# Masked queries of the attentions without rotation: written by ScalarE from the bank, not copied by VectorE

## The chip, the core and the metric

One core of a Trainium2 chip runs the whole program: TensorE (PE), VectorE (DVE), ScalarE (ACT), GpSimd (POOL), SyncE (SP) and the DMA queues. The metric is device time in microseconds (us) of one execution, as the median of several.

## The reference

Four transformer layers over 32 sequences of 128 tokens and 128 features, with a context of the same shape. Each layer is an attention of 16 heads of 8 features and a feed-forward part:

```python
x = x + L0_xattn(layernorm(x), ctx, ctx)   # causal, biases on q, k, v, o
x = x + L0_ffn(layernorm(x))               # 8 experts, top 2, relu
x = x + L1_xattn(layernorm(x), ctx, ctx)   # no mask, biases
x = x + L1_ffn(layernorm(x))               # 8 experts, top 2, gelu
x = x + L2_xattn(layernorm(x), ctx)        # causal self (L2a), then over ctx (L2b), then dense ffn
x = x + L2_ffn(layernorm(x))               # gated: 8 experts that are attentions
x = x + L3_xattn(layernorm(x), ctx, ctx)   # rotated q and k, window of 64
x = x + L3_ffn(layernorm(x))               # 8 experts, top 2, silu gate
```

In each attention `scores = q k^T / sqrt(8)` per head, a softmax, and the weighted sum of v. L0 and L1 have a bias on the query (`q = x Wq + bq`), L2's two attentions have none.

## The kernel before

The 32 sequences are two streams of 16; a stream goes through its sequences in 8 pairs (256 tokens), stage by stage: L0 for all pairs, L0's experts over 39 tiles, L1 for all pairs, L1's experts, then for each pair all of L2 and L3's attention, and L3's experts. The program is written by hand for five engines. The steps of both streams are interleaved on every engine in one order, which `choose_order` (L144) makes beforehand from costs and delays that PE's steps yield; each engine then executes in that order without looking ahead. Semaphores release: `filled` of a bank when PE has written it, `taken` of a bank when its last reader is done, and named ones per stream. So an instruction that waits holds back the other stream's work behind it on its engine.

PSUM has eight banks in rings (`RINGS`). The ring "g", banks 4 to 7, serves both streams in turn: projections, the scores of which maxima are taken, sums and transposes; `open_bank` (L340) waits until the bank's last use is taken. 

One attention without rotation (L0, L1, L2a, L2b; 64 in all) runs like this. PE projects the query into one bank ("q"; in L2a the key goes into the same bank). ACT's `queries` (L1083) reads that bank twice: into `qb` in bf16, then into `qf` in f32 (half of the tile `qfs`), and in L2a also the key into `kf`; then the bank is given back. Heads lie in 4 bands of 32 partitions, 4 heads of 8 rows in each. To pick single heads, DVE's `split` (L1384) makes four copies, each times a column of 0 and 1 from `band`: of the key into `km` (bf16, `split_keys`), of the query into `qm` (f32, `begin`). PE's `scores` (L403) multiplies `qb` and `km` into ring g for the maxima that DVE takes (`mx`, L1531); `scores_t` (L426) multiplies `kf` and `qm` into banks 0 to 3, takes the maxima off, and ACT's exps follow. In `attention` (L1563) DVE first waits until the query's bank is taken, copies, and only then goes on to the next step in the order, which as a rule is the other stream's: `tail_turned` and `turned` (tiles `tail_tok`, `h_tok`), `values` (`vaug`), maxima or, in the gated attention, `eq` tiles (L1626).

L3's attention rotates the query on DVE and keeps `qf`, its copies and its semaphores.

Of the kernel before, what the change touches and what calls it, by code (L numbers as in the profile page):

```python
# [100 lines left out]
PROJ = ["L0q", "L0k", "L0v", "L0o", "L1q", "L1k", "L1v", "L1o", "L2q1", "L2k1", "L2v1", "L2q2", "L2k2",  # L101
        "L2v2", "L3q", "L3qs", "L3k", "L3ks", "L3v", "L3o"] + [f"E{m}{p}" for p in range(HP) for m in "qkvo"]
COLS = ["L0q", "L0k", "L1q", "L1k", "L3q", "L3qs", "L3k", "L3ks"] + [f"E{m}{p}" for p in range(HP) for m in "qk"] \
    + [f"f1{c}" for c in range(CH)]
ROWS = ["L0v", "L0o", "L1v", "L1o", "L2v1", "L2v2", "L3v", "L3o", "g1", "be1", "g2", "be2", "g3", "be3",
        "bf2"]
ROUTERS = {0: 0, 1: 1, 3: 2}
# [68 lines left out]
def build(nc, A, out, totals):  # L176
    with ExitStack() as ctx:
# [153 lines left out]
        def _(pe):  # L331
# [8 lines left out]
            def open_bank(ring, *key):  # L340
                i, n = banks.fill(ring, key)
                if w.new(f"taken{i}", n - 1):
                    pe.wait_ge(sem[f"taken{i}"], n - 1)
                return bank[i]
# [4 lines left out]
            def taken(*key):  # L349
                i, n = banks.fills[key]  # L350
                if w.new(f"taken{i}", n):
                    pe.wait_ge(sem[f"taken{i}"], n)

            def stream(s):
# [46 lines left out]
                def attend(k, mask, rot=False, tail=None):  # L401
# [3 lines left out]
                    def scores(b, j):  # L405

                        if b == j == 0:
                            pe.wait_ge(sem[f"keys_ready{s}"], w.next(f"keys_ready{s}"))
                            if rot:
                                pe.wait_ge(sem[f"queries_ready{s}"], w.next(f"queries_ready{s}"))  # L410
                            else:
                                taken(*k, "q")
                        ps = [open_bank("g", *k, "s", b, j + i) for i in range(2)]
                        for i in range(2):
                            r = band_rows(j + i)
                            mm = nc.tensor.matmul(ps[i][:], qb[s][r, seq(b)], km[s][r, :, seq(b)], start=True,  # L416
                                                  stop=mask is None)
                            if mask is None:
                                filled(mm, *k, "s", b, j + i)
                        if mask is not None:  # L420
                            for i in range(2):
                                filled(nc.tensor.matmul(ps[i][:], identb[:, 0, :], masks[:, 2 * mask, :].unsqueeze(1)  # L422
                                                        .to_broadcast([P, HB, P]), start=False, stop=True),
                                       *k, "s", b, j + i)

                    def scores_t(b):  # L426
                        if b == 0:
                            pe.wait_ge(sem[f"split_ready{s}"], w.next(f"split_ready{s}"))
                        ps = [open_bank("t", *k, "sT", b, j) for j in range(BANDS)]
                        for j in range(BANDS):  # L430
                            nc.tensor.matmul(ps[j][:], kf[s][band_rows(j), seq(b)], qm[s][band_rows(j), :, seq(b)],  # L431
                                             start=True, stop=False)
                        if mask is not None:
                            for j in range(BANDS):
                                nc.tensor.matmul(ps[j][:], identb[:, 0, :], masks[:, 2 * mask + 1, :].unsqueeze(1)
                                                 .to_broadcast([P, HB, P]), start=False, stop=False)
                        for j in range(BANDS):
                            taken(*k, "s", b, j)
                            for i in range(HB):
                                h = HB * j + i  # L440
                                mm = nc.tensor.matmul(ps[j][:, i * P:(i + 1) * P],  # L441
                                                      mx[s][:, b, h:h + 1].to_broadcast([P, P]), identb[:, 1, :],
                                                      start=False, stop=i == HB - 1)
                            filled(mm, *k, "sT", b, j)
# [608 lines left out]
        def _(act):  # L1053
# [12 lines left out]
            def stream(s):  # L1066
# [15 lines left out]

                def queries(k, name, bias, rot=False, keys_too=False):  # L1083
                    ps = take(*k, "q")
                    if not rot:
                        shifted(qb[s][:], ps[:, 0:NT], name if bias else None)
                    ins = shifted(qf[s][:], ps[:, 0:NT], name if bias else None)
                    if rot:
                        ins = shifted(qs[s][:], ps[:, NT:2 * NT], name + "s" if bias else None)
                    if keys_too:  # L1090
                        ins = shifted(kf[s][:], ps[:, NT:2 * NT], None)
                    give(ins, *k, "q")

                def exp(i, last_read, *key):
# [204 lines left out]
        def _(dve):  # L1299
# [35 lines left out]
            def stream(s):  # L1335
# [218 lines left out]
                    yield "unit"  # L1554
                    divide(1)

                def begin():
                    split(qm, qf).then_inc(sem[f"split_ready{s}"], 1)

                def split_keys():  # L1560
                    split(km, kf).then_inc(sem[f"keys_ready{s}"], 1)

                def attention(k, x, bias, rot=False, tail=None):  # L1563
                    taken(*k, "q")
                    if rot:
                        rotate(qf)
                        nc.vector.tensor_copy(qb[s][:], qf[s][:]).then_inc(sem[f"queries_ready{s}"], 1)
                    begin()
                    yield "q"
                    yield from attend(k, tail)  # L1570
                    yield "unit"
                    settle(nc.vector.tensor_tensor(x[:], x[:], row(bias), ALU.add))
                    yield "att"
                    ps = take(*k, "out")
                    settle_given(nc.vector.tensor_tensor(x[:], x[:], b2(ps[:, 0:NT]), ALU.add), *k, "out")
                    norm(x, 1)
                    yield "out"
# [150 lines left out]
                for i in range(PAIRS):  # L1728
# [7 lines left out]
                    turned(x)  # L1736
                    yield "turns"
                    values(k, "L2v1")
                    taken(*k, "q")
                    split_keys()  # L1740
                    begin()
                    yield "q"
                    yield from attend(k, tail)
                    settle(nc.vector.tensor_tensor(hh[:], h[:], att_tok[s][:], ALU.add))
# [6 lines left out]
                    yield "kv"  # L1751
                    turned(hh, gain=row("g1"), shift=row("be1"))
                    yield "turn"
                    taken(*k, "q")
                    begin()
                    yield "q"
                    yield from attend(k)
                    settle(nc.vector.tensor_tensor(hh[:], h[:], att_tok[s][:], ALU.add))
# [46 lines left out]
def laid_out(i):  # L1805
# [28 lines left out]
        col[f"Eq{e}"], col[f"Ek{e}"] = pairs(f["L2_ffn_qb"])[e], pairs(f["L2_ffn_kb"])[e]  # L1834
    for c in range(CH):
        col[f"f1{c}"] = f["L2_xattn_bf1"][c * P:(c + 1) * P]
    row = {"L0v": f["L0_xattn_bv"], "L0o": f["L0_xattn_bo"], "L1v": f["L1_xattn_bv"], "L1o": f["L1_xattn_bo"],
           "L2v1": f["L2_xattn_bv1"].reshape(P), "L2v2": f["L2_xattn_bv2"].reshape(P), "L3v": f["L3_xattn_v_b"],
           "L3o": f["L3_xattn_o_b"], "bf2": f["L2_xattn_bf2"]}
# [35 lines left out]
        .astype(np.float32)  # L1875
    own = np.arange(P)[:, None] // D % NE == np.arange(NE)[None, :]
    a["vbias"] = np.where(own[:, None, :], pairs(f["L2_ffn_vb"]).T[:, :, None], 0.0).astype(np.float32)
    a["band"] = (np.arange(P)[:, None] % 32 // D == np.arange(HB)[None, :]).astype(np.float32)
    a["tri"] = (np.arange(NE)[None, :] < np.arange(NE)[:, None]).astype(np.float32)
    for n in (0, 1, 3):  # L1880
        a[f"moe{n}"] = a[f"moe{n}"].reshape(NE * P, -1)
# [25 lines left out]
```

## Time and profile before

| | |
|---|---|
| time, 3 runs | 3804.05, 3807.44, 3823.59 us; median 3807.44 |
| profiled execution | 3820.63 us; its span 3818.7 us |
| PE / DVE / ACT / POOL busy | 2878.4 / 2028.2 / 1361.3 / 639.8 us |
| L0, both streams: period of a pair of each | 47.6 us (copies at 252.15 and 299.74) |
| L1, the same | 50.4 us (copies at 849.34 and 899.70) |
| L2, gated attention and L3, the same | 279.9 us (copies at 2004.61 and 2284.50) |

The profile is of one execution on the only core. The timeline lists instructions in order of their start in microseconds, merges neighbours of a kind with a count, and says in brackets how long the engine had been idle before and what released it. Rows of LDWEIGHTS are not used.

### The profile page before, as it was taken

The numbers are of one execution on the slowest core, as the hardware profiler recorded it, in microseconds if no ns is written. First come the engines' busy times: TensorE is split into PE (matmuls) and PEld (weight loads), VectorE is DVE, ScalarE is ACT, GpSimd is POOL, SyncE is SP. The second block draws the span as 40 slices with busy tenths as digits, with TensorE's granted clock in tenths as the row PEclk, the third lists the DMA queues.
The fourth block names the chain that finished last, engine by engine and source line by source line (L and its number), as shares of the span: only waits on it lengthen the run. The fifth ranks groups of instructions, "written<-read, shape, count | busy, mean of one in ns | idle before, by whom it ended". The sixth has DMA issues, their size and how long they took to land. (4 is left out here: it accounts for less than half of the span.)

```text
span 3818.7 us, 62592 instructions
## 1 busy us (share of the span) xinstructions
PE 2878.4 (75%) x23570; PEld 2120.4 (56%) x23570; DVE 2028.2 (53%) x6834; ACT 1361.3 (36%) x3026; POOL 639.8 (17%) x853
## 2 busy tenths in 40 slices
PE   5887867665777877878878878878878878959453
PEld 2344646533565755746746746746646646738352
DVE  3566344466444356656656556556656566554411
ACT  1333323232554733323323324324334333327210
POOL 1122111233211011111111111111111111110303
PEclk8778989876988988978979979979879889879776
DMA  6201535300544500000000000000000000014353
GB/s 231 100 23 49 175 120 173 103 25 23 179 145 146 156 9 7 2 8 7 2 8 7 2 9 5 3 8 5 4 10 2 4 9 2 2 36 128 96 144 102
DMA packets 146506, 216.98 MB, mean 57 GB/s; under 512 B 20376, under 2 KB 99232, under 8 KB 146080
## 3 DMA queue, kind: packets, MB, share of 16 engines
q1 hardware_dynamic: 133920, 187.79, 16.2%
q0 software_dynamic: 12288, 25.19, 2.3%
q8 instruction: 190, 3.11, 0.3%
q14 instruction: 108, 0.88, 0.1%
HBM read 159.82 MB, written 53.08 MB: 56 GB/s over the span
## 5 line engine op out<-in xcount | busy, mean ns | idle before, releaser
L1099 ACT ACTIVATE ex<-bank 128x512 f32<-128x512 f32 x896 | 483.3, 601 | 675.6 <-PE bank L441 453.1
L1531 DVE TENSOR_REDUCE mx<-bank 128x4 bf16<-128x512 f32 x640 | 406.7, 684 | 82.8 <-PE bank L422 44.4
L927 POOL TENSOR_TENSOR rstd<-vare,power 128x2 f32<-128x2 f32 x192 | 138.6, 722 | 1378.9 <-DVE vare L1350 1378.4
L936 POOL DMA_INDIRECT sent<-tail_tok,pos x192 | 192.4, 1002 | 601.2 <-DVE pos L1472 557.9
L368 PE MATMUL bank<-hT,wproj 128*128 128x256 f32 x736 | 275.2, 477 | 12.5 <-ACT hT L1069 12.2
L991 POOL TENSOR_TENSOR oT<-oT 128x128 f32<-128x128 f32 x256 | 118.5, 463 | 952.3 <-DVE oT L1644 952.2
L524 PE MATMUL bank<-qm,expert 128*128 128x128 f32 x1872 | 273.4, 293 | 2.0 <-ACT ex L1099 1.4
L596 PE MATMUL bank<-ev,ex 128*128 128x65 f32 x2048 | 271.4, 277 | 0.0
L596 PEld LDWEIGHTS bank<-ev,ex 128*128 128x128 f32 x2048 | 263.9, 196 | 6.1
L524 PEld LDWEIGHTS bank<-qm,expert 128*128 128x128 f32 x1872 | 252.5, 209 | 6.4 <-issue 6.2
L358 PE MATMUL bank<-ident,h_tok 128*128 128x128 f32 x224 | 69.0, 406 | 233.1 <-DVE h_tok L1361 124.7
L416 PE MATMUL bank<-km,qb 32*128 32x512 bf16 x640 | 148.5, 473 | 125.1 <-DVE mx L1531 49.2
L532 PE MATMUL bank<-expert,hid 128*128 128x128 f32 x1560 | 232.1, 291 | 5.7 <-ACT ex L1099 3.3
L431 PE MATMUL bank<-qm,kf 32*128 32x512 f32 x1280 | 217.4, 740 | 22.8 <-ACT ex L1099 12.8
L1632 DVE TENSOR_REDUCE emax<-bank 128x4 bf16<-128x512 f32 x256 | 175.2, 687 | 90.1 <-PE bank L571 89.1
L516 PE MATMUL bank<-ident,qm 128*128 128x128 f32 x234 | 77.3, 331 | 191.9 <-DMA qm<-sent 191.4
L580 PE MATMUL bank<-qm,ek 128*128 128x256 f32 x768 | 219.6, 412 | 0.6
L532 PEld LDWEIGHTS bank<-expert,hid 128*128 128x128 f32 x1560 | 210.7, 207 | 9.2 <-ACT ex L1099 6.0
L441 PEld LDWEIGHTS bank<-identb,mx 128*128 128x128 bf16 x2560 | 157.0, 100 | 77.8 <-issue 55.6
L1523 DVE RECIPROCAL rden<-bank 128x16 f32<-128x16 f32 x160 | 41.0, 256 | 279.1 <-PE bank L460 277.4
L451 PE MATMUL bank<-ex,vaug 128*9 128x128 f32 x5120 | 175.9, 275 | 8.6 <-DVE mx L1531 6.4
L358 PEld LDWEIGHTS bank<-ident,h_tok 128*128 128x128 f32 x224 | 29.8, 186 | 266.3 <-DVE h_tok L1361 137.1
(200 smaller groups left out, 5376.4 us busy)
## 6 DMA issues: line engine op xcount, KB each, us to landing
expert<-in_moe SPq DMA_DIRECT2D x78, 578.0 KB, 4.0
expert<-in_moe SPq DMA_DIRECT2D x78, 512.0 KB, 3.8
expert<-in_moe SPq DMA_DIRECT2D x78, 384.0 KB, 3.3
sent<-zeros SPq DMA_DIRECT2D x8, 2560.0 KB, 8.6
qm<-sent SPq DMA_DIRECT2D x234, 64.0 KB, 3.6
answered<-qm SPq DMA_DIRECT2D x234, 64.0 KB, 3.4
ctxT<-ctx_kept SPq DMA_DIRECT2D x32, 128.0 KB, 2.1
wproj<-in_wproj SPq DMA_DIRECT2D x1, 3328.0 KB
```

The source lines that it names most:

```text
L368: mm = nc.tensor.matmul(ps[:, n * NT:(n + 1) * NT], W(weight), src[:], start=True, stop=True)
L431: nc.tensor.matmul(ps[j][:], kf[s][band_rows(j), seq(b)], qm[s][band_rows(j), :, seq(b)], start=True, stop=False)
L441: mm = nc.tensor.matmul(ps[j][:, i * P:(i + 1) * P], mx[s][:, b, h:h + 1].to_broadcast([P, P]), identb[:, 1, :], start=False, stop=i == HB ...
L451: mm = nc.tensor.matmul(ps[32 * i:32 * i + D + 1, j * P:(j + 1) * P], vaug[s][:, b, HB * j + i, :], ex[s][:, j, i, :], start=True, stop=True)
L524: mm = nc.tensor.matmul(ps[:, chunk(c)], expert[s][:, t % SLOTS, chunk(c)], t_turned[s][:, t % 2, :], start=True, stop=True)
L532: mm = nc.tensor.matmul(ps[:, 0:P], t_hid[s][:, t % 2, chunk(c)], expert[s][:, t % SLOTS, 512 + c * P:512 + (c + 1) * P], start=c == 0, st ...
L580: nc.tensor.matmul(out_[:, :, i, :], ek[p % 3][s][:, i, seq(b)], eq[s][p % 3][:, :, seq(b)], start=i == 0, stop=False)
L596: mm = nc.tensor.matmul(ps[:, i * (HE + 1):(i + 1) * (HE + 1)], ex[s][:, u % 4, i, :], ev[s][:, p % 2, b, i % 2, :], start=True, stop=True)
L936: nc.gpsimd.indirect_dma_start(sent[s][:], bass.IndirectOffsetOnAxis(ap=pos[s][:, i, j:j + 1], axis=0), tail_tok[s][:, j // 2, :], None).t ...
L1099: give(nc.scalar.activation(ex[s][:, i], ps[:].rearrange("p (i q) -> p i q", i=4), ACT.Exp, scale=SCALE), *key)
L1531: give(nc.vector.tensor_reduce(mx[s][:, b, HB * i:HB * i + HB], ps[:].rearrange("p (i k) -> p i k", i=HB), AX.X, ALU.max), *k, "s", b, i)
L1632: give(nc.vector.tensor_reduce(emax[s][:, u % 4, :], ps[:].rearrange("p (i k) -> p i k", i=4), AX.X, ALU.max), *k, "s", u)
```

## The change

In `queries` without rotation ACT writes `qb` first and signals `queries_ready`, then writes the four masked queries `qm` itself from the bank: each an ACTIVATE with a column of `band` as per-partition scale, in L0 and L1 with a bias that is masked the same way (eight new columns of constants, `L0q0` to `L1q3`), in L2 as Copy with a scale. The bank is given back after the fourth. In L2a the key is read first. DVE's copies of the query and its wait for the bank go; in L2a DVE waits for `queries_ready` before it copies the key. PE's first scores wait for `queries_ready`, and `scores_t` for the bank to be taken.

```diff
@@ PE, scores and scores_t
-                            if rot:
-                                pe.wait_ge(sem[f"queries_ready{s}"], w.next(f"queries_ready{s}"))
-                            else:
-                                taken(*k, "q")
+                            pe.wait_ge(sem[f"queries_ready{s}"], w.next(f"queries_ready{s}"))
...
-                        if b == 0:
+                        if b == 0 and rot:
                             pe.wait_ge(sem[f"split_ready{s}"], w.next(f"split_ready{s}"))
+                        elif b == 0:
+                            taken(*k, "q")
@@ ACT, queries
                     ps = take(*k, "q")
-                    if not rot:
-                        shifted(qb[s][:], ps[:, 0:NT], name if bias else None)
-                    ins = shifted(qf[s][:], ps[:, 0:NT], name if bias else None)
                     if rot:
-                        ins = shifted(qs[s][:], ps[:, NT:2 * NT], name + "s" if bias else None)
+                        shifted(qf[s][:], ps[:, 0:NT], name)
+                        give(shifted(qs[s][:], ps[:, NT:2 * NT], name + "s"), *k, "q")
+                        return
                     if keys_too:
-                        ins = shifted(kf[s][:], ps[:, NT:2 * NT], None)
+                        shifted(kf[s][:], ps[:, NT:2 * NT], None)
+                    shifted(qb[s][:], ps[:, 0:NT], name if bias else None).then_inc(sem[f"queries_ready{s}"], 1)
+                    for h in range(HB):
+                        if bias:
+                            ins = nc.scalar.activation(qm[s][:, h, :], ps[:, 0:NT], ACT.Identity, bias=col(f"{name}{h}"),
+                                                       scale=band[:, h:h + 1])
+                        else:
+                            ins = nc.scalar.activation(qm[s][:, h, :], ps[:, 0:NT], ACT.Copy, scale=band[:, h:h + 1])
                     give(ins, *k, "q")
@@ DVE, attention
-                    taken(*k, "q")
+                    w.next(f"queries_ready{s}")
                     if rot:
+                        taken(*k, "q")
                         rotate(qf)
                         nc.vector.tensor_copy(qb[s][:], qf[s][:]).then_inc(sem[f"queries_ready{s}"], 1)
-                    begin()
+                        split(qm, qf).then_inc(sem[f"split_ready{s}"], 1)
@@ DVE, L2a
-                    taken(*k, "q")
+                    dve.wait_ge(sem[f"queries_ready{s}"], w.next(f"queries_ready{s}"))
                     split_keys()
-                    begin()
@@ DVE, L2b
-                    taken(*k, "q")
-                    begin()
+                    w.next(f"queries_ready{s}")
```

How the order moves, at three places (`filled5`: bank 5 written, `taken5`: bank 5 given back). On ACT in the L0 stage, both streams: a query of one stream and the load of the other, before:

```order
L1069 ACTIVATE attT<-bank 128x256 [waits filled6]
L1069 ACTIVATE hT<-bank 128x256 [waits filled7]
L1074 ACTIVATE qb<-bank,cols 128x256 [waits filled5]
L1074 ACTIVATE qfs<-bank,cols 128x256
L1069 ACTIVATE ctxT<-bank 128x256 [waits filled6,ctx_kept0]
L1074 ACTIVATE kf<-bank,cols 128x256 [waits filled7]
```

and now:

```order
L1068 ACTIVATE attT<-bank 128x256 [waits filled6]
L1068 ACTIVATE hT<-bank 128x256 [waits filled7]
L1073 ACTIVATE qb<-bank,cols 128x256 [waits filled5]
L1093 ACTIVATE qm<-bank,cols,band 128x256 x4
L1068 ACTIVATE ctxT<-bank 128x256 [waits filled6,ctx_kept0]
L1073 ACTIVATE kf<-bank,cols 128x256 [waits filled7]
```

One instruction has become four, ahead of the other stream's ctxT. On DVE in the L1 stage, both streams: the tail and the query of stream 0, then the same of stream 1 and its first maxima, before:

```order
L1356 TENSOR_SCALAR h_tok<-x_tok,mv,rstd 128x128
L1386 TENSOR_SCALAR qm<-qfs,band 128x256 [waits taken4,ln_ready0]
L1386 TENSOR_SCALAR qm<-qfs,band 128x256 x3
L1356 TENSOR_SCALAR tail_tok<-x_tok,mv,rstd 128x128 [waits rstd_ready1,scattered1]
L1356 TENSOR_SCALAR tail_tok<-x_tok,mv,rstd 128x128
L1356 TENSOR_SCALAR h_tok<-x_tok,mv,rstd 128x128 [waits rstd_ready1]
L1356 TENSOR_SCALAR h_tok<-x_tok,mv,rstd 128x128
L1531 TENSOR_REDUCE mx<-bank 128x4 [waits filled7,ln_ready1]
L1531 TENSOR_REDUCE mx<-bank 128x4 [waits filled4]
L1386 TENSOR_SCALAR qm<-qfs,band 128x256 [waits taken5]
L1386 TENSOR_SCALAR qm<-qfs,band 128x256 x3
L1531 TENSOR_REDUCE mx<-bank 128x4 [waits filled7]
```

and now:

```order
L1361 TENSOR_SCALAR h_tok<-x_tok,mv,rstd 128x128
L1361 TENSOR_SCALAR tail_tok<-x_tok,mv,rstd 128x128 [waits rstd_ready1,scattered1,ln_ready0]
L1361 TENSOR_SCALAR tail_tok<-x_tok,mv,rstd 128x128
L1361 TENSOR_SCALAR h_tok<-x_tok,mv,rstd 128x128 [waits rstd_ready1]
L1361 TENSOR_SCALAR h_tok<-x_tok,mv,rstd 128x128
L1536 TENSOR_REDUCE mx<-bank 128x4 [waits filled7,ln_ready1]
L1536 TENSOR_REDUCE mx<-bank 128x4 [waits filled4]
L1536 TENSOR_REDUCE mx<-bank 128x4 [waits filled7]
```

Both sets of copies and both waits for a query's bank (taken4, taken5) are gone from between the two streams' work. PE's instructions stand as before; only the semaphores of the first scores and of `scores_t` differ. One place of it in the L2 stage now, where stream 1's query (L2b) goes into bank 5 and two pairs of stream 0's L3 scores follow:

```order
L358 MATMUL bank<-ident,h_tok 128x128 [waits taken4,ln_ready1]
L358 MATMUL bank<-ident,h_tok 128x128
L368 MATMUL bank<-hT,wproj 128x256 [waits taken5,taken4]
L413 MATMUL bank<-km,qb 128x512 [waits taken7,taken6]
L413 MATMUL bank<-km,qb 128x512
L419 MATMUL bank<-masks,identb 128x512 x2
L413 MATMUL bank<-km,qb 128x512 [waits taken5]
L413 MATMUL bank<-km,qb 128x512
```

The same rows stood there before: the second pair of scores waits for bank 5, which the query holds.

## Rows read from the trace of the kernel before

**Rows 1.** Cores: span and mean granted TensorE clock.
```profile
core 0: 3818.7 us, clock 0.853
```

**Rows 2.** Windows (bounds, length; busy us and instructions by engine; PEclk, DMA share, GB/s): L1, L2.
```profile
750.00:950.00 200.00, 119.87 (x1224) 76.03 (x1222) 133.34 (x490) 60.40 (x130) 63.64 (x69) 0.71 0.08 23
...
1953.00:2233.00 280.00, 228.57 (x1831) 167.38 (x1830) 168.61 (x548) 97.19 (x210) 41.88 (x64) 0.87 0.02 6
```

**Rows 3.** Groups (busy us, mean ns | idle before, releasers): the query copies on DVE.
```profile
L1386 DVE TENSOR_SCALAR qm<-qfs,band 128x256 f32<-128x256 f32 x320 | 91.8, 351 | 80.1 <-ACT qfs L1074 48.7 <-ACT qfs L1073 31.3
```

**Rows 4.** One tile (ns min/median/max, first and last start, form): ACT's bf16 query.
```profile
L1074 ACT ACTIVATE qb<-bank,cols x32: 474/474/475, 36.4 to 1111.3; 128x256 bf16<-128x256 f32 x32
...
L1073 ACT ACTIVATE qb<-bank x32: 384/384/384, 1149.8 to 3362.9; 128x256 bf16<-128x256 f32 x32
```

**Rows 5.** Timeline (start, us, instruction, count [idle before <-releaser]), L0, both streams.
```profile
298.86 0.47 ACT L1074 ACTIVATE qb<-bank,cols 128x256 bf16<-128x256 f32 x1 [1.32 <-PE bank L368]
...
299.24 0.47 ACT L1074 ACTIVATE qfs<-bank,cols 128x256 f32<-128x256 f32 x1
...
299.59 0.38 ACT L1069 ACTIVATE ctxT<-bank 128x256 f32<-128x256 f32 x1
...
299.74 1.14 DVE L1386 TENSOR_SCALAR qm<-qfs,band 128x256 f32<-128x256 f32 x4 [0.23 <-ACT qfs L1074]
...
300.03 1.22 PE L368 MATMUL bank<-ctxT,wproj 128*128 128x256 f32 x2 [0.78 <-ACT ctxT L1069]
```

**Rows 6.** Timeline, L0, one stream alone: the first scores.
```profile
104.54 0.61 PE L416 MATMUL bank<-km,qb 32*128 32x512 bf16 x2 [0.98 <-issue]
```

**Rows 7.** Timeline, ACT, L0, the other attention of the period.
```profile
269.92 2.07 ACT L1099 ACTIVATE ex<-bank 128x512 f32<-128x512 f32 x4 [3.29 <-PE bank L441]
```

**Rows 8.** Timeline, L0 beside the other stream's expert tiles.
```profile
451.34 0.47 ACT L1074 ACTIVATE qb<-bank,cols 128x256 bf16<-128x256 f32 x1 [0.73 <-PE bank L368]
...
455.43 0.33 PE L516 MATMUL bank<-ident,qm 128*128 128x128 f32 x1 [0.85 <-DMA qm<-sent]
```

**Rows 9.** Timeline, L1, both streams.
```profile
898.75 0.47 ACT L1074 ACTIVATE qb<-bank,cols 128x256 bf16<-128x256 f32 x1 [1.31 <-PE bank L368]
...
899.70 1.14 DVE L1386 TENSOR_SCALAR qm<-qfs,band 128x256 f32<-128x256 f32 x4 [3.49 <-ACT qfs L1074]
...
901.40 0.69 PE L358 MATMUL bank<-ident,tail_tok 128*128 128x128 f32 x2 [2.69 <-DVE tail_tok L1356]
...
902.54 0.61 PE L416 MATMUL bank<-km,qb 32*128 32x512 bf16 x2
...
904.34 0.47 ACT L1074 ACTIVATE qb<-bank,cols 128x256 bf16<-128x256 f32 x1 [1.31 <-PE bank L368]
...
906.27 1.28 DVE L1531 TENSOR_REDUCE mx<-bank 128x4 bf16<-128x512 f32 x2
```

**Rows 10.** Timeline, PE: waits for maxima behind a full DVE queue.
```profile
1162.40 0.61 PE L416 MATMUL bank<-km,qb 32*128 32x512 bf16 x2 [7.03 <-DVE mx L1531]
...
1366.40 0.39 PE L416 MATMUL bank<-km,qb 32*128 32x512 bf16 x2 [0.78 <-DVE mx L1531]
```

**Rows 11.** Timeline, L2b beside the other stream's L3.
```profile
1963.79 0.38 ACT L1073 ACTIVATE qb<-bank 128x256 bf16<-128x256 f32 x1 [1.31 <-PE bank L368]
...
1965.19 0.61 PE L416 MATMUL bank<-km,qb 32*128 32x512 bf16 x2
```

**Rows 12.** Timeline, L2a beside the other stream's dense layer.
```profile
2002.83 1.95 PE L736 MATMUL bank<-wf,hid 128*128 128x128 f32 x16
...
2005.66 0.41 DVE L1768 TENSOR_TENSOR hh_tok<-hh_tok,bank 128x256 f32<-128x256 f32 x1
...
2007.82 0.39 PE L416 MATMUL bank<-km,qb 32*128 32x512 bf16 x2 [1.80 <-DVE mx L1531]
```

**Rows 13.** Timeline, L2b beside the start of the gated attention.
```profile
2038.09 0.38 ACT L1073 ACTIVATE qb<-bank 128x256 bf16<-128x256 f32 x1 [0.58 <-PE bank L368]
...
2038.85 1.14 DVE L1386 TENSOR_SCALAR qm<-qfs,band 128x256 f32<-128x256 f32 x4 [0.72 <-ACT qfs L1073]
...
2040.80 0.39 PE L416 MATMUL bank<-km,qb 32*128 32x512 bf16 x2 [0.89 <-DVE qm L1626]
```

More of the change, by code:

```diff
@@ L103 @@
 COLS = ["L0q", "L0k", "L1q", "L1k", "L3q", "L3qs", "L3k", "L3ks"] + [f"E{m}{p}" for p in range(HP) for m in "qk"] \
-    + [f"f1{c}" for c in range(CH)]
+    + [f"f1{c}" for c in range(CH)] + [f"{n}{i}" for n in ("L0q", "L1q") for i in range(HB)]
 ROWS = ["L0v", "L0o", "L1v", "L1o", "L2v1", "L2v2", "L3v", "L3o", "g1", "be1", "g2", "be2", "g3", "be3",
@@ L1555, in attend @@
                     divide(1)
-                def begin():
-                    split(qm, qf).then_inc(sem[f"split_ready{s}"], 1)
                 def split_keys():
@@ L1836, in laid_out @@
         col[f"f1{c}"] = f["L2_xattn_bf1"][c * P:(c + 1) * P]
+    in_band = np.arange(P)[:, None] % 32 // D == np.arange(HB)[None, :]
+    for n in ("L0q", "L1q"):
+        for h in range(HB):
+            col[f"{n}{h}"] = np.where(in_band[:, h], col[n], 0.0).astype(np.float32)
     row = {"L0v": f["L0_xattn_bv"], "L0o": f["L0_xattn_bo"], "L1v": f["L1_xattn_bv"], "L1o": f["L1_xattn_bo"],
@@ L1877, in laid_out @@
     a["vbias"] = np.where(own[:, None, :], pairs(f["L2_ffn_vb"]).T[:, :, None], 0.0).astype(np.float32)
-    a["band"] = (np.arange(P)[:, None] % 32 // D == np.arange(HB)[None, :]).astype(np.float32)
+    a["band"] = in_band.astype(np.float32)
     a["tri"] = (np.arange(NE)[None, :] < np.arange(NE)[:, None]).astype(np.float32)
```

## Prediction

> **What bounds the kernel now.** I read the core's span and clock first, then the costliest groups, the windows by stage, and last the timeline of all engines around every one of the 64 attentions without rotation (16 each of L0 and L1, 32 of L2). The span is 3818.7 us at a granted clock of 0.853 [rows 1], the execution took 3820.63 us. The windows say that no engine is full: in L1's stage TensorE (PE) is busy 60% and VectorE (DVE) 67%, in one period of the L2 stage 82% and 60%, ScalarE (ACT) only 30 to 35% [rows 2]. So the time is a chain that changes engines, and what an instruction is worth depends on whether the chain passes it. The four query copies on DVE are 320 instructions in all, 256 of them without rotation; DVE sat idle 80.1 us waiting for ACT's query before them [rows 3]. That wait blocks what is queued behind it for the other stream; this, more than the copies' length, is what the change can win.
>
> **Prices.** Four DVE copies in a row take 1.14 us [rows 5]; the change takes 64 such rows away, 73 us of DVE's time. On ACT one output of 128x256 takes 474 ns with a bias operand and 384 ns without [rows 4]. Neighbours overlap by 0.10 us: the bank's second reader starts 0.38 us after the first, not 0.47 [rows 5]. A copy with a per-partition scale and bias stands nowhere in this trace. An operand costs at most what the bias row shows, 90 ns, and at least nothing; I take 90 ns for each, being the nearest row: 0.56 us for a copy in L0 and L1 (steps of 0.46), 0.47 us in L2 (steps of 0.37). From the start of the first output to the end of the last read of the query's bank, L0 and L1 go from 0.37 + 0.47 = 0.84 us to 0.37 + 3 x 0.46 + 0.56 = 2.31 us, **1.47 us more**; L2 from 0.28 + 0.38 = 0.66 to 0.28 + 3 x 0.37 + 0.47 = 1.86 us, **1.20 us more**. With operands for nothing these are 1.11 and 0.84, with no overlap about 1.9 and 1.6. ACT gets about 85 us of work. The order of the work, the bank ring and all DMAs stay; eight more columns of constants are loaded once and count as nothing behind the other loads.
>
> The Trainium skill (ScalarE: Activation LUTs, What ACT_TABLE_LOAD costs) says each per-partition pointer operand adds about 93 ns to an ACTIVATE. By it the copies come out within a few hundredths of a microsecond of mine, and the sum within 1 us; no row here has two such operands.
>
> **The 64 places, by pattern.** (a) Single-stream L0, 4 times. PE waits for the whole query before its first scores [rows 6]; now it waits for the bf16 copy alone, 0.37 us earlier, and the masked copies are done before its second pair. **-1.5 us.**
>
> (b) L0 with both streams, the attention followed by the other stream's load, 4 times. ACT's ctxT evacuation stands right behind the query, and PE already waits 0.78 us for it [rows 5]. It goes back by 1.47 us; all that follows (keys, the key copies on DVE, the maxima, the other stream's tail_tok for which PE waits) hangs on it. The DVE time freed there buys nothing, since DVE waits for PE next. **+5.9 us.**
>
> (c) The other L0 attention of that period, 4 times: ACT has 3.29 us free before its next exps [rows 7], and PE runs without a gap. Nothing.
>
> (d) L0, L1 and L2 beside the other stream's expert tiles, 7 times: PE's next tile waits for its rows by DMA until 455.43; ACT's delayed tile evacuation is done before that (the query starts at 451.34, + 2.31 + 0.28 = 453.9) [rows 8]. If that cover were gone, each would cost up to 1.47 us. Nothing.
>
> (e) L1 with both streams, 3 periods. DVE waits 3.49 us for ACT's query, copies, and only then makes tail_tok and h_tok for the other stream, for which PE has waited 2.69 us [rows 9]. Now DVE makes them at once. What is late next is the query's bank: the ring of four comes round to it with the first scores. It is returned at 898.75 + 2.31 + 0.1 = 901.2 against 902.54 before, so 1.4 us are won. Then the second query, at 904.34 before and now near 903.1, no longer puts its copies ahead of the maxima at 906.27, which can start near 904.0 when their scores are there; PE next waits for the second query's bank, returned at 903.1 + 2.4 = 905.5. In all 2.1 us are won per period. **-6.3 us.**
>
> (f) A saturated DVE queue with PE waiting for maxima at its end, 3 times (two of them stand in [rows 10], the third is like the first): the copies come off in full, -1.14 us twice, or as far as the wait goes, -0.8 us. **-3.1 us.** Four attentions in odd places at the ends of stages I read as -0.7, +0.5 and -0.4 together: **-0.6 us.** The rest of the L1 places are covered by these or by (d).
>
> (g) L2b beside the other stream's L3 scores, 8 times. DVE's copies are hidden. The fourth score bank after the query is the query's own: it comes back at 1963.79 + 1.86 + 0.1 = 1965.75, and PE wanted it at 1965.19 [rows 11]. This is a new wait of PE on ACT with exps and maxima behind it. **+4.5 us.**
>
> (h) L2a beside the dense layer, 7 times. DVE's four copies end where it takes hh_tok at 2005.66. Without them it takes it at about 2005.0, 0.2 us after PE's dense product is done (2002.83 + 1.95); the maxima for which PE waits 1.80 us come 0.7 us sooner [rows 12]. **-4.9 us.**
>
> (i) L2b beside the start of the gated attention, 7 times. The copies at 2038.85, after another wait of 0.72 us on ACT, hold back the other stream's eq tile of L1626, for which PE waits 0.89 us [rows 13]. Now PE is bound by the query's bank, 2038.09 + 1.86 + 0.1 = 2040.05 against 2040.80: **-5.2 us.**
>
> (j) L2a inside the gated attention, 7 times, and the L2 places before the steady state: the copies stood between maxima that PE reaches later, and ACT is free. Nothing.
>
> **The sum:** -1.5 + 5.9 - 6.3 - 3.1 - 0.6 + 4.5 - 4.9 - 5.2 = **-11.2 us**, from 3820.63 to 3809.4. The profiled execution is 13.2 us above the median of the runs shown, so I put the median at 3807.44 - 11.2 = **3796 us**. With operands for nothing (b) is 4.4, (g) 1.6, (e) -7.4 and (i) -7.7: -19 us. Without overlap they are 7.5, 7.7, -5.0 and -2.4: -2 us.
>
> **Rivals.** *More comes back than the waits.* PE's clock fell in the stretches with DVE waits: 0.71 in the L1 window [rows 2], where a pair of score matmuls takes 0.61 us [rows 9] against 0.39 us at the upper of the two levels (1.2 and 2.4 GHz) [rows 13]. PE was idle for 2.69 us before those slow ones, and it is at the upper level where it had run without such a gap. If fewer gaps let a third of the 120 us of PE's busy time in that window run at the upper level, that is another 120 / 3 x 0.36 = 14 us, -26 us in all, 3781 us. For it: -2.1 us falls on the very gap before the slow rows. Against: most of the gaps stay (DVE maxima and gates), and (b) and (g) open new ones. Chance 0.22.
>
> *ACT becomes the path; slower.* The query's bank is held 1.2 to 1.47 us longer, in a ring of four that both streams share, and every evacuation behind it is late. I count 12 places where that reaches PE. It decides if it reaches some 30: 30 x 1.35 us = 40, less the 21 us of gains, is +19 us, 3826 us; at all 64 it is +65 us, 3872 us. For it: one wait of this kind is plain in rows 5. Against: ACT is idle two thirds of the time, and I followed each pattern. Chance 0.08. The Trainium skill (ScalarE: Activation LUTs, Rules for kernel authors) says to put multiplies on VectorE, not ScalarE, as VectorE is faster per element; the trace agrees on the speed (four in 1.14 us against my 1.58 to 1.94), and that rule would bring the slower outcome.
>
> *The change wins nothing.* The DVE gains of (e), (h) and (i) are taken by the next wait while (b) and (g) stay: +9 us or less in size, 3808 to 3817 us. For it: in every one of them the bank's return is only 0.7 to 1.4 us ahead of the old time. Chance 0.12.
>
> **How the numbers follow.** The forecast's case, -2 to -19 us, has 0.58. A measurement of this kernel can tell about 0.5% from no change, 19 us. Faster by more than that: the first rival and the tail of the forecast, 0.26. Slower: the second rival, 0.08. Within: 0.66. The range reaches from the first rival, 3779, to 3814, most of the third; about 0.8 lies within.
>
> **What would show it.** Right: DVE's TENSOR_SCALAR qm row falls from 320 to 64, and ACT has 256 new ones of 0.47 and 0.56 us; DVE's wait for qfs (80.1 us) is gone but for the rotated queries; PE's wait of 2.69 us for tail_tok in L1 is replaced by a shorter one for ACT; L1's period (50.4 us) shortens by about 2 us, L0's (47.6 us) lengthens by about 1.5 us, L2's (279.9 us) shortens by about 0.9 us. Wrong: copies of another length, an L2 period that moved by more than 3 us, or a clock that moved by over 0.01.

## The result, and the profile after

The changed kernel takes 3779.12 us (median of 5 runs, 3772.20 to 3782.27) against 3808.95 us before; the ratio is 0.991, 95% interval 0.9887 to 0.9933. The gain is 29.8 us between the medians (34 by the ratio), where 11.2 were forecast. The profiled execution took 3772.20 us (before 3820.63), so the traces differ by 48 us, some 19 more than the medians: the profiled execution of before was a long one.

The page of the changed kernel, its busy times (columns as in part 1 of a page):
```profile
span 3770.3 us, 62550 instructions
PE 2832.7 (75%) x23570; PEld 2087.7 (55%) x23570; DVE 1960.6 (52%) x6578; ACT 1443.4 (38%) x3218; POOL 637.2 (17%) x853
```
The cores view and the groups of the copies, changed kernel (busy us, mean ns | idle before, releaser):
```profile
core 0: 3770.3 us, clock 0.865
...
L1391 DVE TENSOR_SCALAR qm<-qfs,band 128x256 f32<-128x256 f32 x64 | 18.1, 347 | 0.0
...
L1093 ACT ACTIVATE qm<-bank,cols,band 128x256 f32<-128x256 f32 x128 | 61.7, 569 | 0.0
L1096 ACT ACTIVATE qm<-bank,band 128x256 f32<-128x256 f32 x128 | 50.2, 482 | 0.2
```
The moved work is as priced: 0.57 and 0.48 us for a copy on ACT (forecast 0.56 and 0.47). DVE lost 256 copies and the 80.1 us wait ahead of them [rows 3]. ACT is 82 us busier, and PE, whose 23570 instructions did not change, is **46 us less busy** at a clock of 0.865 instead of 0.853 [rows 1]. That last line is the surprise.

The places, in the timeline of the changed kernel (start, us, instruction [idle before <-releaser]). L0 with both streams answers to [rows 5]: PE's wait for ctxT went from 0.78 to 2.24 us, +1.46.
```profile
303.03 1.93 ACT L1093 ACTIVATE qm<-bank,cols,band 128x256 f32<-128x256 f32 x4
...
304.83 0.40 ACT L1068 ACTIVATE ctxT<-bank 128x256 f32<-128x256 f32 x1
...
305.28 1.22 PE L368 MATMUL bank<-ctxT,wproj 128*128 128x256 f32 x2 [2.24 <-ACT ctxT L1068]
```
L1 with both streams answers to [rows 9]: PE's 2.69 us wait for tail_tok is gone, and in its place stands one of 1.63 us for the query's bank. From ACT's start on the query to these scores it is 2.44 us instead of 3.79 [rows 9], 1.35 won against 1.34 forecast.
```profile
892.18 0.63 PE L358 MATMUL bank<-ident,tail_tok 128*128 128x128 f32 x2
892.43 0.47 ACT L1073 ACTIVATE qb<-bank,cols 128x256 bf16<-128x256 f32 x1 [1.31 <-PE bank L368]
...
892.80 1.93 ACT L1093 ACTIVATE qm<-bank,cols,band 128x256 f32<-128x256 f32 x4
...
894.87 0.61 PE L413 MATMUL bank<-km,qb 32*128 32x512 bf16 x2 [1.63 <-ACT qm L1093]
```
The three places of L2, for [rows 11], [rows 12] and [rows 13]: a new wait of 0.43 us, then 1.00 instead of 1.80 us, then 0.20 instead of 0.89 us.
```profile
1937.05 0.60 PE L413 MATMUL bank<-km,qb 32*128 32x512 bf16 x2 [0.43 <-ACT qm L1096]
...
1977.91 0.42 DVE L1769 TENSOR_TENSOR hh_tok<-hh_tok,bank 128x256 f32<-128x256 f32 x1 [0.24 <-PE bank L735]
...
1980.08 0.39 PE L413 MATMUL bank<-km,qb 32*128 32x512 bf16 x2 [1.00 <-DVE mx L1536]
...
2012.45 0.80 PE L413 MATMUL bank<-km,qb 32*128 32x512 bf16 x4 [0.20 <-ACT qm L1096]
```
Each of these places moved as forecast, to within 0.15 us. The sum did not. To see where it failed I set the two traces side by side at the 192 rstd instructions of POOL, which are the same in both, and took the time from one to the next:

| stage, in the time of before | forecast | changed kernel less before | five runs without a change in L0 or L1, less before |
|---|---|---|---|
| 0 to 161, L0, one stream | -1.5 | -0.4 | -2.4 to +1.8 |
| 161 to 348, L0, both | +5.9 | **+6.0** | -1.6 to +0.5 |
| 348 to 736, beside expert tiles | 0 | -5.5 | -4.4 to -1.6 |
| 736 to 946, L1, both | -6.3 | -9.6 | -2.2 to +0.7 |
| 946 to 1353, beside expert tiles; L2 begins | up to -3.7, (f) and odd places | -10.2 | -9.8 to -1.8 |
| one L2 period (279.9) | -0.9 | **-4.4 or -2.4 in turn** | (L2 was changed in them) |
| 3403 to the end, no attention without rotation | 0 | -4.1 | -6.6 to +3.3 |

The last column (runs e5, e6, e15_s0, e15_s1 and e16, below; from 1150 us on they differ in an L2 attention) shows what a stage varies by with unchanged code: several us beside the expert tiles, where transfers set the pace, and always downwards from the long profiled execution of before. L2's periods vary by 0.3 to 0.4 us at most once they have settled (one of e15_s1 was 3.2 us short), so there the 24 us over seven periods are real. Windows over two L2 periods, from the same rstd instruction to itself two periods on, first before, then changed:
```profile
2007.16:2566.95 559.79, 456.95 (x3660) 334.80 (x3660) 337.03 (x1093) 194.40 (x420) 84.02 (x128) 0.87 0.02 6
```
```profile
1979.42:2532.37 552.95, 449.35 (x3660) 329.61 (x3660) 329.44 (x1061) 203.88 (x444) 83.57 (x128) 0.89 0.02 6
```
The pair of periods is 6.84 us shorter. PE's busy time (second number) fell by 7.60 us with the same 3660 instructions, its idle time rose by 0.76. What L2 gained is faster matmuls; over the whole period its waits did not get shorter.

### The profile page after: what moved, and what is told of

It is laid out like the page before. It is cut to its first block and busy times, and to the rows that moved or that the text cites. A ratio compares the mean times of both kernels' runs of the same rounds, so it can differ in the third digit from the quotient of the medians.

```text
span 3770.3 us, 62550 instructions
## 1 busy us (share of the span) xinstructions
PE 2832.7 (75%) x23570; PEld 2087.7 (55%) x23570; DVE 1960.6 (52%) x6578; ACT 1443.4 (38%) x3218; POOL 637.2 (17%) x853
## 5 line engine op out<-in xcount | busy, mean ns | idle before, releaser
L368 PE MATMUL bank<-hT,wproj 128*128 128x256 f32 x736 | 263.5, 459 | 14.1 <-ACT hT L1068 13.8
L523 PEld LDWEIGHTS bank<-qm,expert 128*128 128x128 f32 x1872 | 244.4, 203 | 6.4 <-issue 6.1
L440 PE MATMUL bank<-identb,mx 128*128 128x128 bf16 x2560 | 179.6, 226 | 0.0
```

The source lines that it names most:

```text
L368: mm = nc.tensor.matmul(ps[:, n * NT:(n + 1) * NT], W(weight), src[:], start=True, stop=True)
L440: mm = nc.tensor.matmul(ps[j][:, i * P:(i + 1) * P], mx[s][:, b, h:h + 1].to_broadcast([P, P]), identb[:, 1, :], start=False, stop=i == HB ...
L523: mm = nc.tensor.matmul(ps[:, chunk(c)], expert[s][:, t % SLOTS, chunk(c)], t_turned[s][:, t % 2, :], start=True, stop=True)
```

## The experiments

Two theories. **Places**: the time is the sum of the waits at the places of the prediction. **Clock**: a small saving also lets PE run more of its work at the upper of its two levels, and this decides. The runs were made in groups, each on one chip beside its own runs of before: e1 to e4, e5 to e8, e9 with e12, e13 to e15, and e16. Gains of a run in us are its ratio times the time of before, unless a trace is named. The snippets are shortened, and names such as `wproj_248_columns` stand for longer expressions.

**Stages apart (e1, e2, e3).** A condition on the layer decides on all engines whether the masked queries come from ACT or, as before, from DVE:
```diff
+BY_ACT = ("L0", "L1")                 # e2: ("L2a", "L2b"); e3: ("L1", "L2a", "L2b")
-    if rot:                            # DVE, attention()
+    if k[2] not in BY_ACT:
         taken(*k, "q")
+        begin()                        # the four copies
```


> The change in L0 and L1 alone (128 of the 256 copies on ACT); L2's attentions as before. By the places of the prediction: -1.5 + 5.9 - 6.3 - 3.1 - 0.6 = -5.6 us against before (ratio 0.9985). By the theory that TensorE's clock gives back more at many places in every stage (the traces of the two kernels differ by 20 us at 1353 us): -10 to -20 us (0.997 to 0.995), with L2's period back at 279.9 us.

> The change in L2 alone (the other 128 copies). By the places of the prediction: +4.5 - 4.9 - 5.2 = -5.6 us (0.9985), an L2 period of 279.0 us. By the clock theory: L2's period falls by about 3.5 us as in the changed kernel, -17 to -24 us (0.9955 to 0.9935), and PE's busy time in a period falls by as much as the period, while its idle time stays.

> The change in L1 and L2, L0 as before. If the late ctxT evacuation of L0 with both streams costs what the prediction and the trace say (+5.9 us less the 1.5 us won in single-stream L0), this is 4.4 us faster than the changed kernel: 3775 us, ratio to before 0.990. If L0's stage beside expert tiles gained on its own (the traces say up to -7 us from 380 to 736 us), it is 0 to 3 us slower than the changed kernel.

L0 and L1 alone: 0.9986 (0.9976 to 0.9997), -5.3 us where the places say -5.6. L2 alone: 0.9933 (0.9919 to 0.9947), -25.5 us where they say -5.6. The parts add up to the whole. Without L0: 0.9901 (0.9884 to 0.9918), in the direction of the 4.4 us that L0 costs, though the interval reaches the changed kernel; the trace is clearer: stage 161 to 348 is 6.0 to 6.4 us longer in e1, e7 and both traces of the changed kernel (4.5 in e4), and +0.4 us in e3. So L0 and L1 were read right, and a term of L2 is far off.

**DVE's wait or DVE's copies (e4, e7).** e4 keeps a wait of DVE on ACT's query, e7 keeps copies:
```diff
+    dve.wait_ge(sem[f"queries_ready{s}"], n)        # e4: where taken(*k, "q") stood
```
```diff
+    for i in range(HB):                             # e7: where the copies stood, no wait
+        nc.vector.tensor_scalar(spare[:, s, i, :], wproj_248_columns, band[:, i:i + 1], None, ALU.mult)
```


> The changed kernel, but DVE still waits for ACT's bf16 query at the place where it waited before; no copies on DVE. If DVE's blocking wait carries the gain (the prediction's L1 places), most of it goes: 0 to -8 us against before, L1's period back near 50 us. If the 73 us of copies carry it, most stays: -20 us or more against before, with L2's period as in the changed kernel (276.5 us). By the places of the prediction about 4 us of its 11 go.

> The changed kernel with four DVE products of 128x248 (inputs constants, outputs read by nobody) put where the query's copies were, without a wait: 256 instructions, about 73 us of DVE. If the copies' time carries the gain, most of it goes: 0 to -10 us against before, L2's period back near 279 us. If DVE's blocking wait carried it, the kernel stays at -25 us or better. With the run in which DVE still waits (0.9923) this splits the gain in two.

e4's wait ends with ACT's first output, a little sooner than the wait of before, which was for the bank; and in L2a the changed kernel has it anyway, so e4 tests L0, L1 and L2b. e7's products are of 128x248 instead of 128x256, without a wait. With the wait kept the kernel is at 0.9923 (0.991 to 0.9937): nearly the whole gain stays. With the copies back it is at 0.9975 (0.9958 to 0.9992), and two L2 periods take 559.5 to 559.9 us: L2's gain is gone (PE's wait at the place of [rows 12] is back at 1.70 us). The copies carry it. In L1 either is enough: its stage was 5.9 us shorter in e4 and 7.6 in e7, against 5.3 to 9.6 in runs with both; behind the first relief waits the query's bank.

**Which attention of L2 (e5, e6), which stream (e15).** The same condition, on L2a, on L2b, and on L2a of one stream.

> The change in L2's first attention alone (16 of 64 attentions). By the prediction's places: -0.7 us in each of 7 periods and nothing inside the gated attention, -4.9 us (ratio 0.9987), period 279.2 us. If the step of -1.1 and -2.9 us that the changed kernel shows at the first attention inside the gated one is this attention's own, -2 to -2.7 us per period: -14 to -19 us (0.996 to 0.995). If it is only TensorE's clock answering to the whole period's pattern, no half of the change alone need show its share.

> The change in L2's second attention alone. By the prediction's places: +4.5 - 5.2 = -0.7 us (1.000), period 279.8 us, with the new wait of 0.4 to 0.5 us of PE for the query's bank. If the two halves add up to the 3.45 us per period of the whole, it takes what the other run leaves: -5 to -11 us. If the clock makes it, the halves do not add up, and PE's idle time in a period is within 1 us of before in both.

> The change in L2's first attention of stream 0 alone (8 of 64 attentions). If the place beside the dense layer decides, the stream that has it gives the whole step (two periods 552.9 us, -24 us, ratio 0.9935) and the other nothing. If both places count the same, each gives half of it (556.4 us, -12 us, 0.997).

> The same for stream 1 alone. With its neighbour it adds up to the run of both streams (0.9931) if the two places count by themselves; by a step theory the sum need not hold, and each is 0, -12 or -24 us.

L2a alone: 0.9931 (0.9911 to 0.9951), all of L2's gain. L2b alone: 0.9997 (0.9986 to 1.0008), -1 us, where the places say -0.7. In stream 0 L2a stands beside the other stream's dense layer: 0.9929 (0.9912 to 0.9945). In stream 1 it stands inside the gated attention: 0.9997 (0.9986 to 1.0009). **Eight attentions out of 64, 32 copies, suffice for the whole step**, and they are the places of [rows 12], priced at 0.7 us each. In run e15_s0 the place itself gave just that (1.00 us of waiting against 1.80):
```profile
1991.80 0.42 DVE L1794 TENSOR_TENSOR hh_tok<-hh_tok,bank 128x256 f32<-128x256 f32 x1 [0.24 <-PE bank L739]
...
1993.97 0.39 PE L417 MATMUL bank<-km,qb 32*128 32x512 bf16 x2 [1.00 <-DVE mx L1547]
```
The rest came later in the same period, where no instruction had been changed. Windows of 4 us, kernel before (the number behind the five engines is PEclk):
```profile
2178.00:2182.00 4.00, 2.17 (x18) 1.74 (x16) 2.65 (x9) 1.14 (x3) 0.45 (x1) 1.00 0.00 0
2182.00:2186.00 4.00, 2.02 (x7) 1.41 (x8) 2.27 (x12) 0.77 (x2) 1.16 (x2) 0.61 0.00 0
2186.00:2190.00 4.00, 4.00 (x19) 3.54 (x18) 0.89 (x3) 0.60 (x1) 0.00 (x0) 0.50 0.01 4
2190.00:2194.00 4.00, 4.00 (x17) 3.44 (x17) 1.31 (x5) 1.32 (x4) 0.46 (x1) 0.61 0.01 2
2194.00:2198.00 4.00, 4.00 (x35) 3.26 (x33) 3.29 (x13) 1.58 (x3) 0.45 (x1) 1.00 0.00 0
```
The same stretch in run e15_s0:
```profile
2164.00:2168.00 4.00, 1.54 (x15) 1.26 (x13) 2.58 (x12) 0.98 (x2) 0.05 (x1) 1.00 0.00 0
2168.00:2172.00 4.00, 2.40 (x9) 1.85 (x10) 2.31 (x9) 0.77 (x2) 1.16 (x2) 0.74 0.00 0
2172.00:2176.00 4.00, 4.00 (x28) 3.52 (x27) 0.80 (x3) 1.31 (x4) 0.46 (x1) 0.83 0.01 4
2176.00:2180.00 4.00, 3.89 (x32) 3.22 (x30) 3.71 (x13) 1.67 (x6) 0.00 (x0) 1.00 0.00 0
```
In both PE had been half idle for some 8 us and its clock fell to the lower level (1.2 of 2.4 GHz). Before, it stayed there through one whole window of solid work (0.50) and most of the next (0.61); in e15_s0 it was back in the first third of one (0.83). PE's timeline, before and e15_s0:
```profile
2189.42 1.16 PE L374 MATMUL bank<-wproj,hT 128*128 128x128 f32 x4
2190.38 1.91 PE L368 MATMUL bank<-hT,wproj 128*128 128x256 f32 x4
2192.08 1.06 PE L374 MATMUL bank<-wproj,hT 128*128 128x128 f32 x4
```
```profile
2174.11 0.66 PE L375 MATMUL bank<-wproj,hT 128*128 128x128 f32 x4
2174.61 1.03 PE L369 MATMUL bank<-hT,wproj 128*128 128x256 f32 x4
2175.47 0.61 PE L375 MATMUL bank<-wproj,hT 128*128 128x128 f32 x4
```
The same twelve matmuls took 3.72 us (2189.42 to 2193.14) in the one and 1.97 (2174.11 to 2176.08) in the other, with no wait in either; with their neighbours ahead this stretch gave 2.4 us. A second of this kind, near 2130, gave 1.1 us. With the 0.74 us of the place these make 4.2. Some 0.8 us went back later, partly in longer waits of PE and partly where matmuls came out at the lower level instead: 3.4 us are left, the period's gain. Two periods of e15_s0, to be held against those of before shown above:
```profile
1993.31:2546.24 552.93, 449.25 (x3660) 327.73 (x3660) 334.87 (x1085) 196.56 (x426) 83.59 (x128) 0.90 0.02 6
```
Per period PE is 3.85 us less busy and 0.4 us more idle: the time saved at the place comes back as idle time elsewhere, and the whole gain is in PE's busy time. That the saving is what brought the clock up sooner is inferred from the edit, which touched nothing else; the link between the two was not isolated.

**How the saving turns into time (e9, e12).** e9 puts 1, 2 or 3 idle copies back into L2a alone; e12 is e3 (L0 as before) and gives L2b's bank back early:
```diff
+    for i in range(1):                              # 2, 3; DVE, L2a only, behind split_keys()
+        nc.vector.tensor_scalar(spare[:, s, i, :], wproj_248_columns, band[:, i:i + 1], None, ALU.mult)
```
```diff
+    give(shifted(qf[s][:], ps[:, 0:NT], None), *k, "q")        # e12: ACT, L2b
+    act.wait_ge(sem[f"taken{i}"], n)
+    ... nc.scalar.activation(qm[s][:, h, :], qf[s][:], ACT.Copy, scale=band[:, h:h + 1])
```


> The changed kernel with one idle DVE product of 128x248 (0.33 us) back in each of L2's first attentions. So far L2's period was 279.9 us or 276.5 us in the mean of two, whatever was changed, and nothing between. If the period follows the path (linear theory), four products make 3.4 us and one makes 0.85: 277.3 us. If it moves in one step between two values, it is 276.5 or 279.9 us, here most likely 276.5.

> Two idle products in each of L2's first attentions. Linear theory: 278.2 us. Step theory: 276.5 or 279.9 us in the mean of two periods, and a run time that differs from the neighbour's by 0 or by some 24 us.

> Three idle products in each of L2's first attentions. Linear theory: 279.0 us. Step theory: 276.5 or 279.9 us; once the step has come, a further product costs nothing.

> L0 as before, the change in L1 and L2; in L2's second attention ACT first writes the query's bf16 and f32 forms, gives the bank back (as early as before) and makes the four masked copies from the f32 form. It takes away the new wait of PE for the query's bank (0.43 us, with 1.0 us more idle time per period in the run of L2b alone) and adds 0.28 us to ACT. Linear theory: 1 us per period less than in the kernel without L0, -8 us: 3763 us. Step theory: the period stays at 276.5 us (same time as without L0, 0.990), or goes down a further step of 3.4 us to 273.1 us (-24 us, 0.984).

Two periods of L2 took 556.4 us with one idle copy, 559.8 with two, 559.8 with three. Neither theory as put held: the period is not linear in the work, nor does it have only two values. Nor does it follow the wait that was saved. At the place of [rows 12] PE waited 1.00 us with one idle copy, as with none, 1.18 with two and 1.44 with three, against 1.80 before. Here e9_copies1, then e9_copies2:
```profile
2040.43 0.39 PE L414 MATMUL bank<-km,qb 32*128 32x512 bf16 x2 [1.00 <-DVE mx L1537]
```
```profile
2033.65 0.39 PE L414 MATMUL bank<-km,qb 32*128 32x512 bf16 x2 [1.18 <-DVE mx L1537]
```
The idle copies stand in L2a of both streams, so with one of them the loss must come from elsewhere in the period; where was not followed up. Windows over two periods of e9_copies1, then e9_copies2:
```profile
2039.77:2596.17 556.40, 454.07 (x3660) 332.46 (x3660) 329.80 (x1065) 203.66 (x444) 83.58 (x129) 0.88 0.02 6
```
```profile
2032.99:2592.80 559.81, 457.31 (x3660) 334.53 (x3660) 330.70 (x1069) 204.00 (x444) 83.68 (x129) 0.87 0.02 6
```
The ratios follow: 0.9946 (0.9925 to 0.9967), 0.9983 (0.9973 to 0.9994), 0.9986 (0.9973 to 0.9999); one product of 0.34 us costs half the step, the second the other half, the third nothing. e12 also came out at 556.4 us and 0.993 (0.9914 to 0.9946): taking a wait of 0.43 us away and adding 0.28 us of ACT work did not give a microsecond per period but, against e3's 552.95 us, took half a step back. Over all runs, two settled periods took:

| two periods, us | kernels |
|---|---|
| 559.8 (559.5 to 560.1) | before, e1, e6, e7, e9_copies2, e9_copies3, e15_s1, e16 |
| 556.4 | e9_copies1, e12 |
| 552.9 to 553.2 | changed kernel (twice), e2, e3, e4, e5, e8, e14, e15_s0 |

**Control, and the leanest version (e13, e14).** e9 and e12 ran on a chip whose kernel before took 3851 us, not 3803 to 3810. e13 is the changed kernel unaltered, on another chip; e14 has BY_ACT = ("L1", "L2a").

> The changed kernel once more, as the control of its neighbours. If the chip has no part in the steps, two of L2's periods make 552.9 us again; if the chip decides, 556.4 us or another value, and the ratio to before moves from 0.991.

> The change in L1 and in L2's first attention alone; L0 and L2b as before. It leaves out the two places with a new wait of PE (L0 with both streams, L2b beside the L3 scores). By the steps: two periods of L2 at 552.9 us, ratio near the kernel without L0 (0.990) and 1 us better than it for the L2b wait if that is on the path; next step down: 0.984.

e13: 0.9922 (0.9908 to 0.9936), two periods 552.9 us. The slower chip loses its time ahead of L2 (its two periods of 559.8 us in e9 agree with the others within 0.03 us), so the middle value is probably those kernels' own; the changed kernel itself was not run on that chip. e14: 3775.26 us, 0.991 (0.9892 to 0.9928), beside e13's 3778.66: as good with half of the copies moved, and not measurably better. e3 has the lowest ratio, 0.9901. No version beats the changed kernel beyond the intervals.

**Filling PE's idle time (e8), moving the copies (e16).**
```diff
     for i in range(2):                              # e8: PE, scores()
         ps.append(open_bank("g", *k, "s", b, j + i))
+        if i == 0:
+            nc.tensor.matmul(ps[0][:], identb[:, 0, :], mask_512_columns, start=True, stop=True)
```
```diff
     split_keys()                                    # e16: DVE, kernel before, L2a, stream 0
-    begin()
     yield "q"
+    begin()
```


> The changed kernel with one more product on PE (128x512 bf16, overwritten at once) between the openings of the two score banks of a pair, 320 in all, where PE mostly waits for DVE's maxima. It removes no wait and only fills idle time. If the granted clock decides, it rises above 0.867 and the matmuls behind those waits come out at the upper level: 5 to 40 us faster than the changed kernel. If the clock has no part in it, the kernel is slower by what is not hidden, 0 to 320 x 0.21 = 67 us.

> The kernel before, with all 320 copies on DVE, but in L2's first attention of stream 0 they stand behind the step of the other stream that follows instead of ahead of it. If the 0.7 us at that place decide, the period falls by 3.4 us here too (two periods 552.9 us) and the run is near 0.993, as with the copies on ACT. If DVE's load decides (9 us of copies per stream), nothing changes: 1.000, period 279.9 us.

e8 raised the clock, to 0.869 against 0.865, and was 0.998 (0.9968 to 0.9993): some 25 us slower than the changed kernel. Two L2 periods took 552.95 us all the same, with 8.5 us more of PE's busy time and as much less idle; the loss is in the other stages. A higher clock, bought with this work on PE, did not pay. e16: 1.0011 (0.9999 to 1.0022), no gain. Behind the other stream's step the copies still stand ahead of L2a's maxima, and PE's wait there was 2.01 us, not shorter than 1.80:
```profile
1999.74 0.39 PE L416 MATMUL bank<-km,qb 32*128 32x512 bf16 x2 [2.01 <-DVE mx L1531]
```
This other order does not help; what helped was to take the copies off DVE at that place.

## Why the prediction was wrong

- **Prices**: right. 0.57 and 0.48 us against 0.56 and 0.47; DVE's 256 copies and its wait are gone.
- **(b)** +5.9: right, +6.0 in the stage, +1.46 us of wait at the place against 1.47.
- **(e)** -6.3: right in size, and the next wait was the query's bank, as forecast. The stage gave 5.3 to 9.6 us in the runs with L1 changed, those on the slower chip apart. But the claim that DVE's blocking wait, "more than the copies' length", is what can be won fell: e4 kept a wait on ACT's query and stayed at 0.9923.
- **(a), (d), (f)** and the odd places: L0 and L1 together were -5.3 us against -5.6 forecast. Singly they drown in the scatter of the stages beside expert tiles. At one place near 556 us, by its length the third of (f), priced at -1.14, there is a new wait of 1.26 us for the query's bank that I had not foreseen, ahead of the wait for maxima, which fell from 7.39 to 4.65 us; from ACT's start on the query to the scores behind both it is 7.70 us instead of 8.94, -1.2 us.
- **(g)** +4.5 and **(i)** -5.2: right at the places (0.43 us against 0.56; 0.69 against 0.75), and in sum (e6: -1 us against -0.7).
- **(j)** 0: right (e15_s1, 0.9997).
- **(h)** -4.9, "the maxima for which PE waits 1.80 us come 0.7 us sooner": **the step that failed.** The mechanism and the 0.7 us are right (0.74 measured). What it is worth was mis-sized: the copies in L2a of stream 0 bring 24 us in the trace of e15_s0 (27 by the ratio, 23 by the medians), about five times 4.9. I let a saving of waiting time count once, at its place; here PE also reached the upper level earlier in two later stretches of the same period, 2.7 us more. With 24 in place of 4.9 the sum is -30 us, and -30 was measured. And e9 shows that pricing by the wait at its place fails in the other direction too: with two idle copies that wait is still 0.6 us shorter than before, and the period gains nothing.
- **The rivals**: the first, that more comes back than the waits, is what happened, at 3779 us against its 3781. The lower end of the range, 3779, was set by it, and the measurement lies right on that end. But I placed it in L1, behind the long waits, and gave it 0.22; it came in L2, whose clock of 0.87 looked healthy. Both signs that I had named for a wrong forecast came: L2's period moved by 3.4 us, the clock by 0.012. The second rival, ACT as the path, did not come: ACT went from 36% to 38% busy. The Trainium skill (ScalarE: Activation LUTs, Rules for kernel authors) puts multiplies on VectorE as the faster engine per element. The traces agree on the speed (four copies in 1.14 us on DVE, 1.93 on ACT in L0 and L1), but not on where these copies belong: with them on the slower engine the kernel is faster. The third, that the next waits eat the gains, holds for L1's second relief alone.

## What to carry to other kernels

Where PE alternates between its two levels within a loop, a wait saved need not be worth its own length: find the stretches in which solid work runs at the lower level, count them as up for winning or losing, and widen the range by them. Split a change by place before you judge it: here eight attentions of 64 sufficed for most of the gain, and one layer cost time. And compare the lengths of settled periods, not whole traces, whose stages with transfers differ by several us between runs of the same code.

## What was not expected of the hardware

- Two settled periods of L2 took 559.8, 556.4 or 552.9 us in 19 traces of 18 kernels, apart from a few tenths, whatever the edit. Between kernels with the same length, PE's busy and idle time trade: in e6 the new wait of L2b put 2.1 us more idle time into two periods (559.80 in all) and the clock took 2.1 us of busy time out. What sets the spacing of 3.4 us is left open.
- The clock's return can be early or late by several us after much the same half-idle stretch: 0.61, 0.50, 0.61 before, 0.74, 0.83 in e15_s0. What decides it was not isolated.
- An ACT output of 128x256 with a scale and a bias operand takes 0.57 us, with the scale alone 0.48, with a bias alone 0.47, with neither 0.38: each operand adds about 0.09 us. The Trainium skill (ScalarE: Activation LUTs, What ACT_TABLE_LOAD costs) says that each such pointer operand adds about 93 ns, and the trace agrees, for one and for two at once.
